# Two buffers for the transposed q and k, and the pair's final sum written in two halves around the transposes

## What is computed

```python
ada = t_emb @ w_ada + b_ada
sh_msa, sc_msa, g_msa, sh_mlp, sc_mlp, g_mlp = jnp.split(ada, 6, axis=-1)
xn = layer_norm(logmap0(x))
xm = expmap0(xn * (1 + sc_msa) + sh_msa)
q = _to_heads(plin(xm, w_q, b_q))          # k, v alike; 16 heads of 16
qt, kt, vt = (logmap0(q), logmap0(k), logmap0(v))
attn = jax.nn.softmax(jnp.einsum('bhqd,bhkd->bhqk', qt, kt) / math.sqrt(HD), axis=-1)
out_h = expmap0(jnp.einsum('bhqk,bhkd->bhqd', attn, vt))
attn_out = plin(_from_heads(out_h), w_o, b_o)
x = mobius_add(residual, expmap0(g_msa * logmap0(attn_out)))
xn = layer_norm(logmap0(x))
xm = expmap0(xn * (1 + sc_mlp) + sh_mlp)
ff = plin(plin(xm, w_f1, b_f1), w_f2, b_f2)
return x0 + mobius_add(residual, expmap0(g_mlp * logmap0(ff)))
```

## Time and profile before

| | us |
|---|---|
| median of 3 runs | 774.34 |
| lowest and highest | 772.27, 775.95 |
| the profiled execution | 778.25 |
| its span, from the first instruction to the last | 776.2 |
| PE busy | 650.5 |
| DVE busy | 657.1 |
| ACT busy | 521.6 |
| POOL busy | 341.3 |

### The profile page before, as it was taken

How to read it: one execution, slowest core, us unless ns; L and a number is a source line. 1 busy time by engine, 2 the same in 40 slices (tenths; PEclk the granted TensorE clock), 3 DMA queues, 4 the chain that set the end, 5 groups by cost and what they waited for, 6 DMA issues and landing times. The chain is left out here.

```text
span 776.2 us, 27058 instructions
## 1 busy us (share of the span) xinstructions
PE 650.5 (84%) x8419; PEld 466.0 (60%) x8433; DVE 657.1 (85%) x2171; ACT 521.6 (67%) x1563; POOL 341.3 (44%) x683
## 2 busy tenths in 40 slices
PE   4956889999999998999999997506869999999996
PEld 2645667777777776777677775403336656656664
DVE  1877789999999999999999996586898998998975
ACT  1123567777777777777777775335768888888884
POOL 1002556666666666666666664111243233323321
PEclk9978799999999999999999998557899999999999
DMA  9942576666676666666666664313435445545523
GB/s 320 358 114 63 123 141 136 152 137 148 135 147 142 143 140 145 137 147 134 147 133 141 143 130 97 71 39 97 125 91 150 148 125 163 155 121 160 163 71 108
DMA packets 184804, 107.50 MB, mean 138 GB/s; under 512 B 140188, under 2 KB 167591, under 8 KB 184744
## 3 DMA queue, kind: packets, MB, share of 16 engines
q1 hardware_dynamic: 182952, 103.99, 54.5%
q10 hardware_dynamic: 1792, 2.89, 1.0%
HBM read 64.11 MB, written 9.18 MB: 94 GB/s over the span
## 5 line engine op out<-in xcount | busy, mean ns | idle before, releaser
L875 PE MATMUL p_qkv<-wqkv,tT 128*128 128x256 f32 x768 | 198.2, 396 | 5.5 <-DVE u L1129 5.5
L875 PEld LDWEIGHTS p_qkv<-wqkv,tT 128*128 128x128 f32 x768 | 140.0, 195 | 23.0 <-issue 6.3
L889 PEld LDWEIGHTS p_o<-v,pT 64*64 64x64 f32 x4096 | 67.3, 137 | 22.2 <-issue 22.2
L889 PE MATMUL p_o<-v,pT 64*64 64x17 f32 x4096 | 73.6, 210 | 0.0
L497 POOL TENSOR_TENSOR rt<-ss,c_mhalf 128x2 f32<-128x2 f32 x32 | 23.9, 747 | 106.2 <-ACT wqkv L700 106.2
L848 PE MATMUL p_oz<-wo,oT 128*128 128x256 f32 x256 | 69.7, 397 | 0.0
L438 POOL TENSOR_TENSOR rt<-ss_t,c_mhalf 128x1 f32<-128x1 f32 x64 | 42.1, 658 | 60.6 <-ACT junk L627 53.7
L652 ACT ACTIVATE pT<-p_s 128x1024 f32<-128x1024 f32 x64 | 65.5, 1023 | 3.0 <-PE p_s L865 1.9
L1129 DVE SCALAR_TENSOR_TENSOR u<-p_qkv,ct,bqkv 128x768 f32<-128x768 f32 x64 | 64.3, 1005 | 3.4 <-PE p_qkv L875 3.4
L610 ACT ACTIVATE oT<-p_oz 128x256 f32<-128x256 f32 x64 | 24.5, 383 | 56.6 <-PE p_oz L840 56.6
L937 PE MATMUL p_qkv<-wff,qk 128*128 128x384 f32 (+1 forms) x128 | 58.9, 608 | 3.7 <-ACT qk L712 3.6
(11 more groups left out here) (273 smaller groups left out, 1672.4 us busy)
## 6 DMA issues: line engine op xcount, KB each, us to landing
mod<-mod_rows SPq DMA_DIRECT2D x128, 128.0 KB, 2.9
x_all<-in_x SPq DMA_DIRECT2D x8, 1024.0 KB, 14.1
gate<-mod_rows SPq DMA_DIRECT2D x128, 64.0 KB, 2.7
mod<-mod_rows SPq DMA_DIRECT2D x32, 256.0 KB, 4.2
mod_b<-mod_rows SPq DMA_DIRECT2D x32, 256.0 KB, 4.4
out<-x_all SPq DMA_DIRECT2D x32, 256.0 KB, 3.0
gate<-gate_rows SPq DMA_DIRECT2D x32, 128.0 KB, 2.9
bqkv<-gate_rows SPq DMA_DIRECT2D x32, 128.0 KB, 2.9
```

What stands on the lines that cost most here:

```text
L875: mm = pe.matmul(p_qkv[:, a * D:a * D + D], tT[:, k, c, :], wqkv[:, c, a * D:a * D + D], start=c == 0, stop=c == C - 1)
L889: mm = pe.matmul(p_o[S * e:S * e + S, col:col + VW], pT[keys, e, g, :], v[keys, k, 2 * g + e, :], start=True, stop=True, skip_group_check= ...
```

## The change

The DMA transpose of odd tiles goes to a second buffer, which lies in the last four tiles of `g_all`, free until the attention stage writes them. SP no longer waits for the previous scores, but for the last tile, which goes to the first buffer. The landing semaphore is one for each buffer. `gate_z` of the last four tiles waits until the scores no longer read the second buffer. In the MLP stage `add_up` and `diagonals` take one tile of the pair at a time: PE transposes between the two halves of the sum, and ACT makes the first tile's two diagonals ahead of `evac_t2T` and the other two behind it.

```diff
+        qkTs = (qkT[:, :, :, :], g_all[:, T - 4:T, :].rearrange("p t d -> p (t d)").bitcast(F16).rearrange(
+            "p (a g n) -> p a g n", a=2, g=G))
...
+        def last_tile(h, off, lag):
+            return isinstance(h, int) and 2 * h + off - lag == T - 1
...
                     sp.wait_ge(again_ready, 2 * i + 2)
-                    after(sp, s_psum, i)
+                    if last_tile(h, off, L_H):
+                        sp.wait_ge(s_psum, i)
                     sp.sem_inc(rows_begun, 1)
-                    sp.dma_start(qkT[:, :, :, :].rearrange("p a g n -> p (a g) n"),
-                                 qk4s[k].rearrange("p a h r d -> p (a h r d)"), transpose=True).then_inc(qkT_in, 16)
+                    sp.dma_start(qkTs[0 if last_tile(h, off, L_H) else k].rearrange("p a g n -> p (a g) n"),
+                                 qk4s[k].rearrange("p a h r d -> p (a h r d)"), transpose=True).then_inc(qkT_in[k], 16)
...
+                if i >= T - 4:
+                    dve.wait_ge(s_psum, T - 2)
...
+                if on_sum(h, off, M_D):
+                    diagonals(slots - M_D, 0, *diag_of)
                 if group_at(h, off, M_P) is not None:
                     tanh_norm(group_at(h, off, M_P))
                 if on2(h, off, M_Q):
                     evac_t2T(slots - M_Q, (off - M_Q) % 2)
                 if on_sum(h, off, M_D):
-                    diagonals(slots - M_D, (off - M_D) % 2, parity(off, M_D), 2 * ((off - M_D) % GROUP),
-                              (TURN // GROUP) * h + (off - M_D) // GROUP)
+                    diagonals(slots - M_D, 1, *diag_of)
...
                 if on_sum(h, off, M_O):
-                    add_up(slots - M_O, (off - M_O) % 2, (off - M_O) % TURN)
+                    add_up(slots - M_O, 0, (off - M_O) % 2, (off - M_O) % TURN)
                 if on2(h, off, M_Q):
                     i, k = slots - M_Q, (off - M_Q) % 2
                     transpose_t2(i, k)
+                if on_sum(h, off, M_O):
+                    add_up(slots - M_O, 1, (off - M_O) % 2, (off - M_O) % TURN)
+                if on2(h, off, M_Q):
                     inner_start(i, k)
```

More of the change, by code:

```diff
@@ L235, in build @@
         qk_ready = sem("qk_ready"); high_ready = sem("high_ready"); low_ready = sem("low_ready"); again_ready = sem("again_ready"); v_ready = sem("v_ready")
-        rows_begun = sem("rows_begun"); qkT_in = sem("qkT_in")
+        rows_begun = sem("rows_begun"); qkT_in = [sem(f"qkT_in{k}") for k in range(2)]
         s_psum = sem("s_psum"); p_ready = sem("p_ready")
@@ L462, in scale_v, with low_parts @@
                                    fac[:, 2 * H:3 * H].unsqueeze(2).broadcast_to([P, H, HD]), ALU.mult).then_inc(v_ready, 1)
-            def low_parts(i, k):
+            def low_parts(i, k, half):
                 pool.wait_ge(high_ready, i + 1)
                 pool.wait_ge(qk_ready, 2 * i + 2)
-                after(pool, qkT_in, 16 * (i - 1))
+                after(pool, qkT_in[k], 16 * half)
                 big = qk4s[k]
@@ L599, in _, with high_parts @@
                            p_oz[0:3, D:2 * D].rearrange("p (b n) -> p b n", n=P), ACT.Copy, scale=2.0).then_inc(ffw_made, 1)
-            def high_parts(i, k):
+            def high_parts(i, k, half):
                 act.wait_ge(qk_ready, 2 * i + 2)
-                after(act, qkT_in, 16 * (i - 1))
+                after(act, qkT_in[k], 16 * half)
                 act.activation(qk4s[k][:, :, :, 0, :], qk[:, :].rearrange("p (a h d) -> p a h d", a=2, d=HD), ACT.Copy).then_inc(high_ready, 1)
@@ L728, in tanh_norm, with diagonals @@
                 act.activation(th[:, :], fin[:, 4, :], ACT.Tanh).then_inc(th_ready, 1)
[L730 to L737, removed]
+            def diagonals(i, j, k, q, col, g):
+                if j == 0:
+                    act.wait_ge(al2_ready, g + 1)
+                    act.wait_ge(be2_ready, g + 1)
+                    after(act, out_psum, i - 1)
+                for n, fac2 in enumerate((al2, be2)):
+                    act.activation(diags[k][j][n], ident[:, :], ACT.Copy, scale=fac2[:, q, col + j:col + j + 1]).then_inc(diag_ready, 1)
             def evac_out(i, k):
@@ L751, in slot2 @@
                         clip_rows(slots - M_Q, j, (off - M_Q) % 2)
+                if on_sum(h, off, M_D):
+                    diag_of = ((off - M_D) % 2, parity(off, M_D), 2 * ((off - M_D) % GROUP),
+                               (TURN // GROUP) * h + (off - M_D) // GROUP)
+                    diagonals(slots - M_D, 0, *diag_of)
                 if group_at(h, off, M_P) is not None:
@@ L849, in project_o, with scores_wait, scores @@
                 mm.then_inc(z_psum, 1)
-            def scores_wait(i):
-                pe.wait_ge(qkT_in, 16 * i + 16)
+            def scores_wait(i, k, half):
+                pe.wait_ge(qkT_in[k], 16 * half + 16)
                 after(pe, p_ready, i)
-            def scores(i):
+            def scores(i, rows_of):
                 for g in range(G):
@@ L864, in scores @@
                             col = 512 * e + S * g
-                            mm = pe.matmul(p_s[tok, col:col + S], qkT[rows, 1, g, tok], qkT[rows, 0, g, tok], start=True, stop=True,
+                            mm = pe.matmul(p_s[tok, col:col + S], rows_of[rows, 1, g, tok], rows_of[rows, 0, g, tok], start=True, stop=True,
                                            skip_group_check=True)
@@ L908, in slot @@
                 if on(h, off, L_H):
-                    scores_wait(2 * h + off - L_H)
+                    scores_wait(2 * h + off - L_H, (off - L_H) % 2, h + (off - L_H) // 2)
                 if on(h, off, L_L):
@@ L912, in slot @@
                 if on(h, off, L_H):
-                    scores(2 * h + off - L_H)
+                    scores(2 * h + off - L_H, qkTs[0 if last_tile(h, off, L_H) else (off - L_H) % 2])
                 if on(h, off, L_L):
@@ L939, in inner, with add_up @@
                 mm.then_inc(ff_psum, 1)
[L941 to L952, removed]
+            def add_up(i, j, k, r):
+                pe.wait_ge(diag_ready, 4 * i + 2 * j + 2)
+                if j == 0:
+                    pe.wait_ge(fg_ready, 2 * i + 2)
+                    after(pe, out_ready, i - 1)
+                acc = s_bank[2 + k][:, j * D:j * D + D]
+                xt, x1 = (big[:, bass.ds(2 * i + j, 1), :].rearrange("p a d -> p (a d)") for big in (x_all, g_all))
+                pe.matmul(acc, ident[:, :], xt, start=True, stop=False)
+                pe.matmul(acc, diags[k][j][0], x1, start=False, stop=False)
+                mm = pe.matmul(acc, diags[k][j][1], fgs[r][:, j, :], start=False, stop=True)
+                if j == 1:
+                    mm.then_inc(out_psum, 1)
             def slot2(h, off):
@@ L1204, in scale_qk, with repeat_parts @@
                                       fac[:, a * H:a * H + H].unsqueeze(2).broadcast_to([P, H, HD]), ALU.mult).then_inc(qk_ready, 1)
-            def repeat_parts(i, k):
+            def repeat_parts(i, k, half):
                 dve.wait_ge(high_ready, i + 1)
                 dve.wait_ge(low_ready, i + 1)
-                after(dve, qkT_in, 16 * (i - 1))
+                after(dve, qkT_in[k], 16 * half)
                 q4, k4 = (qk4s[k][:, a, :, :, :].rearrange("p h (y z) d -> p h y z d", y=2) for a in range(2))
```

6 lines of the change are left out of this document (3 added, 3 removed).

## The result

| | before | changed |
|---|---|---|
| median of 5 runs, us | 774.34 | 765.74 |
| lowest, highest | 772.27, 775.95 | 765.42, 767.89 |
| the profiled execution | 778.25 | 765.56 |
| its span | 776.2 | 763.7 |

The ratio is 0.9892, with a 95% interval of 0.987 to 0.9913: 8.6 us less, where 5.7 was forecast.

What follows compares the result with a forecast made beforehand. In the MLP stage PE, ACT and DVE were taken as within a few per cent; in attention DVE was busy 297.86 of 320 us. 2.0 + 1.3 + 2.4 = 5.7 us gave 768.6 (766 to 771.5; 8 in 10: 763.5 to 773.3).

Steps and rivals of the forecast that it cites:

- Steady stretch: Attention stage, steady tiles: transposes start up to 0.3 us earlier, shortening DVE's late `mod` waits; 2.0 us, bounds 0 and 5.3.
- The repeating gap on SP: Attention stage: SP's gap of 1.1 us a tile; by the skill's rule about too few buffers, 5.3 us instead of 2.0.
- End of the stage: Attention stage's last tiles: a transpose no longer held by scores lands earlier for PE; 1.3 us, bounds 1.0 and 2.0.
- The group: MLP stage, four slots with split sum and diagonals: 28.21 us instead of 28.74, a gain of 0.53 to 0.55.
- the walk: Step-by-step timing of PE, ACT and DVE through one MLP group from DVE's late first slot; ends at 28.21 us.
- Six groups: MLP stage: 24 slots have sum and transposes, six groups; 3.3 us gained together.
- The end: MLP stage's last slot with transposes: the second half delays its products by 0.87 us, and nothing following regains it.
- The sum: Whole kernel: 2.0 + 1.3 + 2.4 = 5.7 us less, 768.6 us against the median of 774.34.
- Hidden anyway: Rival, 0.25: new ACT and DVE waits eat the gains; only the attention stage's end and half a microsecond remain, 772.5 us.
- costs more: Rival, 0.05: MLP split regains nothing in the second slot, the 0.45 wait stays in each group; 774.6 us.
- DVE becomes the bound: Rival, 0.10: MLP products come in time and the group falls to 27.1 us; 12.3 us less, 762.0 us.
- Transposes land late: Rival, 0.05: attention-stage transposes take 6.1 us each to land, costing 0.5 us a tile; 796 us.

Runs made afterwards that it cites:

- e4: Against the kernel before: second buffer added, but SP still waits for the previous scores for every tile; MLP part as before. 773.53 us, ratio 1.001.
- e9: Kernel before, one buffer and unsplit sum, with SP issuing a tile's gate transfers a slot later, behind the next mod transfers. 765.31 us, ratio 0.9918.
- e5: Kernel before with the sum split around the transposes on PE alone; all four diagonals stay behind the evacuation. 772.3 us, ratio 0.9991.
- e6: Kernel before with two diagonals moved ahead of the evacuation on ACT alone; PE's sum stays whole ahead of the transposes. 770.08 us, ratio 0.9973.
- e7: Changed kernel with the sum whole again in every fourth slot, the one DVE begins late; diagonals stay split. 763.51 us, ratio 0.9879 to the kernel before.
- e10: Changed kernel run again unaltered, beside its variants. 765.08 us, ratio 0.9909 to the kernel before.
- e1: Kernel before with only the two buffers and the dropped wait for scores; MLP stage as before. 769.94 us, ratio 0.9962.
- e2: Kernel before with only the MLP part, split sum and split diagonals; one buffer as before. 769.63 us, ratio 0.9961.

## Why the prediction was right, point by point

- **Steady stretch, 2.0 forecast, 1.9 measured** as a difference of means, with a standard error of 0.7. The mechanism is shown: e4 (wait kept, no gain), e9 (waits for `mod` gone, 4.7 us less with the wait kept) and the table above. The 4.2 us between the first two traces were no sign of a term that is too small; the row of 5.3 us on which its bounds rested was the highest of seven. So the size was met with some luck: I took 2.5 us from nine waits of a single execution whose size does not repeat. The repeating gap on SP, which the prediction weighed beside the Trainium skill, Perfetto Trace Analysis, Optimization Strategy, would have meant 5.3 us; the kernels gave 1.9, and the prediction's reason for the difference holds: SP is not the engine that is to be saturated.
- **End of the stage, 1.3 forecast, 1.2 measured** (21.1 to 21.2 us in all traces without the wait there, 22.0 to 22.6 with it). The 4.03 us wait became 4.19, not 3.8, since PE's work ahead of it ended earlier as well. The signs on SP came too: between 130 and 460 us its transposes start 0.09 to 0.20 us behind the copy, where it was 0.10 to 0.54.
- **The group, 28.21 forecast, 28.14 measured.** The products start at 3.38 in the late slot and the next transposes at 7.78, as the walk has it (7.79). Behind that, errors of both signs nearly cancel, so the total is closer than its terms. The eight products cost 3.01 to the next matmul where I put 3.11, and DVE could follow 3.21 after their start instead of 3.31; so the waits for them are 0.29 and 0.44, not 0.45 and 0.75, and the second `inner_square` of the third slot comes at 13.21, not 13.29. (The walk's 2.19 from transposes to products should have been 2.22 by its own terms; it was 2.23.) The wait for the root ahead of that slot was to vanish and stayed at 0.23; the wait for the products, which ends later, covers it. From there to the fourth slot it took 6.59, not 6.42: a new wait of 0.34 for a power on POOL (L1415) was not foreseen (e5 and e6 have it too). The fourth slot took 8.34, not 8.50. I had subtracted the idle time of 0.45 that the row of L1407 shows, but from start to start that wait had cost 0.55 (from 626.21 to 626.89, where the changed kernel has 616.60 to 616.73), because without it the instruction begins before the one ahead of it is done; 0.06 more went at the slot's first rows. The walk had both edits arriving at 7.79 together and did not say which of them gains; e5 and e6 show that most is ACT's. The new wait of `evac_out` for the sum is 0.12 us in each of the 24 slots, not 0.2 to 0.3.
- **Six groups, 3.3 forecast, 3.9 measured.** The first, slots 8 to 12, gains 0.86 (28.74 to 27.88), the other five 0.6 each. The walk described only the settled group.
- **The end, 0.87 forecast, 0.2 measured.** This step was wrong. The second inner product's consumer did come later, 743.16 - 736.58 = 6.58 us after the slot's start instead of 755.11 - 749.29 = 5.82, which is 0.76. But I wrote that nothing follows that regains it, and something does: in the last sums, which have no transposes between them, PE no longer waits for all four diagonals but starts the first tile when two are there. ACT's first diagonal and PE's first matmul of the last sums, before:

```profile
766.51 0.40 ACT L737 ACTIVATE z<-ident,al 128x128 f32<-128x128 f32 x1 [1.03 <-DVE al L1427]
...
767.85 0.70 PE L949 MATMUL p_o<-x_all,ident 128*128 128x256 f32 x2
```

and in the changed kernel:

```profile
754.56 0.40 ACT L744 ACTIVATE z<-ident,al 128x128 f32<-128x128 f32 x1 [1.59 <-DVE al L1443]
...
755.31 0.70 PE L959 MATMUL p_o<-x_all,ident 128*128 128x256 f32 x2 [1.21 <-ACT z L744]
```

PE begins 1.34 us behind that diagonal before and 0.75 now, 0.59 less, and from the diagonal to the end of the span it is 776.2 - 766.51 = 9.7 us before and 763.7 - 754.56 = 9.1 now, 0.6 less. So 0.76 lost and 0.6 regained leave the 0.2. e7 confirms it: with the last slot's sum whole but the finer wait kept, the end takes 26.35, which is 26.95 less 0.6.
- **The sum.** 1.9 + 1.2 + 3.9 - 0.2 = 6.8 us by stages, 7.1 by the medians of e10, 8.6 in the first comparison, whose interval begins at 6.7. Up to tile 8 the traces without the wait were 1.1 us earlier on average (141.3 against 142.4), but each group scatters over 2 us or more; whether this is a gain is open.
- **The rivals.** *Hidden anyway* and *costs more* fall with e1 and e2. *DVE becomes the bound* did not come: e7, at 27.91, is still 0.8 above 27.1. *Transposes land late* did not come either: they landed in 4.2 to 6.0 us with a median of 4.3, as before.

## What to carry to other kernels

SP's 79 us of waits were worth about 3 us here; with such a wait, look for what stands behind it in the same queue and who is late for that, and move that ahead before buying a buffer. The Trainium skill, Perfetto Trace Analysis, Optimization Strategy, says to look for the gaps on the engine one optimises and to make what they wait for start sooner; e9 is that, with 6.3 us less by the ratio. Where two engines close one round, filling a hole on the one may gain nothing while the other's is open (e5, 0.01 us a group; e6 0.42; both 0.60), so try each half alone, and don't put a split into the slot that starts late. And cut two traces at the same rows before crediting a stage: here 2 to 5 us of a stage were scatter.

## What was not expected of the hardware

- One program's stages can differ more between executions than the whole does: the two profiled executions of the changed kernel took 765.56 and 765.37 us. From MLP slot 1 to slot 8 the first took 49.59 us and the second 46.89. Windows of that stretch, first run and second:

```profile
540.00:550.00 10.00, 6.75 (x20) 3.04 (x19) 9.86 (x35) 7.16 (x27) 3.12 (x4) 0.93 0.41 117
550.00:560.00 10.00, 7.23 (x20) 3.22 (x18) 7.71 (x32) 5.88 (x23) 4.89 (x4) 0.90 0.26 79
```

```profile
540.00:550.00 10.00, 6.97 (x24) 3.16 (x24) 9.75 (x38) 7.99 (x28) 2.42 (x3) 1.00 0.49 148
550.00:560.00 10.00, 7.18 (x22) 3.16 (x20) 9.27 (x38) 7.49 (x31) 5.58 (x5) 1.00 0.30 89
```

The granted clock was below 1.00 in the one and not in the other, with PE busy for about 7 of 10 us in both. Which of the two came first, the lower clock or the slower work, these rows do not show.
- The eight products took 3.17 where no hole preceded them and 3.27 behind one of 0.26, in the kernels before and changed, e5 and e7. From their start to the next matmul it is 3.01 (599.31 to 602.32) and 3.11, so a hole cost PE 0.1 us beside its own length.
